# Last four token tiles of an attention and routed-spline kernel: one statistics pass, turned signs and keys from TensorE, sums on ScalarE, fp32r limits

## The reference

```
y   = (x1 - mean) / sqrt(var + 1e-5)                 # first norm
xf  = (y - mean(y)) * rsqrt(var(y) + 1e-5) * gamma + beta   # second norm
tile_scores    = sign(xf) @ tile_sigs.T              # 64 tiles of 16 features, signs of mean slopes
cluster_scores = sign(xf) @ cluster_sigs.T           # 8 clusters of 8 tiles
tile_idx = best tile inside the best cluster         # one tile per token
x_slice  = the 16 features of xf in that tile
mn, mx   = min and max of x_slice over ALL tokens that chose the same tile
u   = clip((x_slice - mn) / (mx - mn + 1e-8), 0, 1 - 1e-6)
gi  = int(u * 16)                                    # spline cell, 16 per feature
delta = (bases[tile, j, gi] + slopes[tile, j, gi] * (u * 16 - gi)) * scale[tile]
out = x1 + y, with delta added at the 16 features of the token's tile
```

## Time and profile before

| what | us |
|---|---|
| median of 3 runs | 3238.69 |
| lowest and highest | 3235.26, 3240.01 |
| the profiled execution | 3238.15 |
| its span, first to last instruction | 3236.4 |
| TensorE busy in the span | 3069.6 (95%) |
| VectorE busy | 2083.3 (64%) |
| ScalarE busy | 1490.6 (46%) |
| GpSimd busy | 714.7 (22%) |

### The profile page before, as it was taken

How to read it: one execution, slowest core, us unless ns; L and a number is a source line. 1 busy time by engine, 2 the same in 40 slices (tenths; PEclk the granted TensorE clock), 3 DMA queues, 4 the chain that set the end, 5 groups by cost and what they waited for, 6 DMA issues and landing times.

```text
span 3236.4 us, 39942 instructions
## 1 busy us (share of the span) xinstructions
PE 3069.6 (95%) x13890; PEld 2386.5 (74%) x13890; DVE 2083.3 (64%) x4440; ACT 1490.6 (46%) x2907; POOL 714.7 (22%) x516
## 2 busy tenths in 40 slices
PE   7999999999999999999999999999999999999924
PEld 4788768887788867888678876888678876888722
DVE  2555537775577746777377764777467763777687
ACT  2655525553445435445264543555345452555411
POOL 5222241112211131110411113111311113111046
PEclk9999999999999999999999999999999999999955
DMA  6554444444534445433454444444454444544301
GB/s 205 195 172 160 173 163 164 136 140 148 192 121 140 140 156 189 134 128 130 156 193 140 140 146 172 141 140 140 141 181 140 140 131 150 186 140 137 118 27 4
DMA packets 170054, 473.34 MB, mean 146 GB/s; under 512 B 33136, under 2 KB 61424, under 8 KB 149248
## 3 DMA queue, kind: packets, MB, share of 16 engines
q1 hardware_dynamic: 164784, 469.91, 43.7%
q0 software_dynamic: 5072, 0.88, 0.6%
HBM read 369.84 MB, written 67.31 MB: 135 GB/s over the span
## 4 chain that ended last, share of the span: by engine, by line
PE 83%; DVE 7%; issue 4%; ACT 3%; POOL 2%; DMA 1%; SPq 0%; DVEq 0%; ACTq 0%; POOLq 0%
PE psC L1934 18%; PE psD L1927 10%; PE psA L1864 8%; PE psT L1916 6%; PE psA L1833 5%; PE psB L1873 5%; PE psD L1884 4%; PE psS L1901 3%; PE psB L1833 3%; PE psS L1907 3%; PE psS L1903 3%; PE psS L1902 3%; PE psS L1904 3%; PE psA L1855 2%; PE psB L1855 2%
## 5 line engine op out<-in xcount | busy, mean ns | idle before, releaser
L1934 PE MATMUL psC<-w_o_pair,attn_hi 128*128 128x512 f32 x1920 | 638.4, 413 | 18.7 <-DVE acc L1342 10.8
L1033 ACT ACTIVATE exps_ring<-exps_ring,neg_max 128x512 f32<-128x512 f32 x512 | 370.8, 724 | 424.9 <-DVE neg_max L1314 424.9
L1314 DVE CUSTOM_DVE_ANT_0 exps_ring<-psS,mask 128x512 f32<-128x512 f32 x512 | 353.2, 690 | 294.4 <-PE psS L1907 289.1
L1044 ACT ACTIVATE probsT_hi<-psT 128x512 fp32r<-128x512 f32 x512 | 305.8, 599 | 364.9 <-PE psT L1916 363.3
L1934 PEld LDWEIGHTS psC<-w_o_pair,attn_hi 128*128 128x128 f32 x1920 | 332.2, 189 | 89.5 <-DVE acc L1342 24.9
L1039 ACT ACTIVATE exps_ring<-exps_ring,row_sum_inverse 128x512 f32<-128x512 f32 x512 | 369.6, 722 | 61.0 <-DVE row_sum_inverse L1320 61.0
L1326 DVE TENSOR_TENSOR probsT_lo<-psT,probsT_hi 128x512 fp32r<-128x512 f32 x512 | 350.6, 686 | 58.3 <-ACT probsT_hi L1044 56.6
L1934 PE MATMUL psC<-w_o_pair,attn_lo 128*128 128x512 f32 x960 | 379.4, 395 | 0.0
L1342 DVE TENSOR_TENSOR acc<-acc,psC 128x512 f32<-128x512 f32 x448 | 303.2, 677 | 17.3 <-PE psC L1934 11.4
L1916 PE MATMUL psT<-ident,exps_ring 128*128 128x128 f32 x2048 | 305.0, 272 | 0.0
L1916 PEld LDWEIGHTS psT<-ident,exps_ring 128*128 128x128 f32 x2048 | 252.8, 139 | 66.4 <-issue 2.1
(11 more groups left out here) (301 smaller groups left out, 5497.8 us busy)
## 6 DMA issues: line engine op xcount, KB each, us to landing
w_o_pair<-w_o_split SPq DMA_DIRECT2D x112, 1024.0 KB, 5.4
w_uq_ring<-w_uq_split SPq DMA_DIRECT2D x114, 384.0 KB, 3.5
w_uv_quad<-w_uv_split SPq DMA_DIRECT2D x29, 1024.0 KB, 5.0
w_uk_ring<-w_uk_split SPq DMA_DIRECT2D x114, 256.0 KB, 2.8
w_qr_sorted<-w_qr_split SPq DMA_DIRECT2D x29, 768.0 KB, 4.3
x_stage<-in_x_dram SPq DMA_DIRECT2D x32, 512.0 KB, 5.9
x_stage<-in_ctx_dram SPq DMA_DIRECT2D x32, 512.0 KB, 4.1
acc<-in_x_dram SPq DMA_DIRECT2D x32, 512.0 KB, 5.3
```

The lines of the kernel that those rows point to most:

```text
L1033: act.activation(E[:, qt, :], E[:, qt, :], ACT.Exp, scale=-1.0, bias=mx[:, i % 2, qt:qt + 1], accum_out=rs[:, i % 2, qt:qt + 1]).then_inc( ...
L1044: act.activation(PT[0][:, :, qt * P:(qt + 1) * P], psT[qt % 2][:, :].rearrange("p (c n) -> p c n", c=TT), ACT.Copy)\
L1314: dve.tensor_tensor_reduce(E[:, qt, :], psS[qt % 2][:, :], mask[:, qt, :], -SCALE, BIG, ALU.add, ALU.min, mx[:, i % 2, qt:qt + 1]).then_in ...
L1934: mm_ = pe.matmul(ps[:, :], attn[a][:, 2 * pair + i, t * P:(t + 1) * P], WO[:, half, o, i, :], start=i + a + o == 0, stop=i + a == 2)
```

## The change

All of it is in the ending.

- **One statistics pass.** As the mean of y is 0 and its variance var / (var + eps), both roots together are the power -0.5 of var (1 + eps) + eps². `end_stats` makes both arguments, GpSimd takes both roots in one instruction of two elements and derives bias and scale in two small ones. ScalarE makes the twice normed row without gamma and beta (`end_normed`) straight from `acc`, and later the sum x1 + y (`end_sum`).
- **Signs from turned rows.** TensorE turns the normed row, 8 blocks of 128 features (`end_turn`), and ScalarE takes the sign of each block from PSUM with gamma and beta as per-partition scale and bias (`end_sign`, 8 instructions of 128 columns, bf16). Gamma, beta and the slope signs come as columns (`cols`, three loads of 1024 single elements each, and two small ones for `gbt`), issued by SyncE where the gamma spread was, earlier in the last batch.
- **Keys by TensorE.** `end_keys`: 16 bf16 matmuls of 8 columns with the signs as weights and `wkey` (made by GpSimd) as the moving side give the 64 keys, and VectorE adds the tie numbers and takes the maximum in one instruction. The last four one-hots are turned singly (`end_turn_onehot`), and a small fp32 matmul fetches the chosen tile's gamma and beta (`end_gamma_beta`), which VectorE applies to the 16 chosen features.
- **Order.** TensorE's one-hot turnings stand between the last projections. VectorE does all adds and statistics first, then choices and slices.
- **Limits in fp32r.** `tab` is split into a high and a low part side by side (`tabs`, 8 columns); one fp32r matmul for each token tile, in four groups; VectorE sums the two parts in `place`. Groups 1 to 3 stand between the spline rows.
- **Equality and deltas.** VectorE does the equality of the first four token tiles, ScalarE that of 4 to 7 and of groups 1 to 3. The deltas are finished after 1, 2, 4, 6 and 8 token tiles and then by four.

```diff
+            def end_rstd(t):
+                row = mv4[:, t, :]
+                pool.wait_ge(s_tile[t], 5)
+                pool.tensor_tensor(row[:, 4:6], row[:, 2:4], nhalf[:, :], ALU.pow).then_inc(s_trstd[t], 1)
+                pool.wait_ge(s_trstd[t], 1)
+                pool.tensor_scalar(row[:, 7:9], row[:, 4:6], row[:, 0:1], -1.0, ALU.mult, ALU.mult)\
+                    .then_inc(s_trstd[t], 1)
+                pool.tensor_scalar(row[:, 6:7], row[:, 4:5], 1.0, None, ALU.add).then_inc(s_trstd[t], 1)
...
+            c.do(pool.tensor_copy(blk[:, 0, :], rampi[:, 0:8]))
...
+            pool.wait_ge(s_cols, 80)
+            sign_wide = cols[:, 2, :].rearrange("p (c a) -> p c a", a=1).broadcast_to([P, DB, 8])
+            c.do(pool.tensor_scalar(wkey[:, :, 0, :], sign_wide, 4096.0, None, ALU.mult))
...
+            for t in range(TT):
+                end_rstd(t)
+            for t in range(TT):
+                end_select(t)
...
+            def end_normed(t):
...
+                act.wait_ge(s_trstd[t], 2)
+                act.activation(ends[t][1], acc[:, t, :], ACT.Identity, scale=mv4[:, t, 5:6],
+                               bias=mv4[:, t, 8:9]).then_inc(s_tw, 1)
...
             def end_sign(t):
-                act.wait_ge(s_tile[t], 11)
-                act.activation(ends[t][2], ends[t][1], ACT.Sign).then_inc(s_tsign, 1)
+                act.wait_ge(s_twt, t + 1)
...
+                for blk_ in range(DB):
+                    ps = stages_end[t][blk_ // 4]
+                    act.activation(signs[t % 2][:, blk_, :], ps[:, (blk_ % 4) * P:(blk_ % 4 + 1) * P], ACT.Sign,
+                                   scale=cols[:, 0, blk_:blk_ + 1], bias=cols[:, 1, blk_:blk_ + 1]).then_inc(s_tsign, 1)
...
+            onehot_turned(0, 1, 2, 3)
+            end_normed(0)
+            onehot_turned(4)
+            end_normed(1)
             end_sign(0)
-            onehot_turned(3, 4)
+            onehot_turned(5)
+            end_normed(2)
             end_sign(1)
-            onehot_turned(5, 6)
+            onehot_turned(6)
+            end_normed(3)
             end_sign(2)
+            end_onehot_turned(0)
             end_sign(3)
-            onehot_turned(7)
+            end_onehot_turned(1)
+            end_onehot_turned(2)
+            end_sum(0)
+            end_onehot_turned(3)
+            for t in range(1, TT):
+                end_sum(t)
...
             def end_choose(t):
                 c = ends_c[t]
...
+                dve.wait_ge(s_key, t + 1)
+                c.do(dve.tensor_tensor_reduce(key[:, :], key_bank(t)[:, 0:NT], tie[:, :], -1.0, BIG,
+                                              ALU.add, ALU.min, kmax[:, :]))
+                c.do(dve.tensor_scalar(oh4[:, t, :], key[:, :], kmax[:, 0:1], None, ALU.is_equal))
...
             def end_slice(t):
...
+                c.do(dve.tensor_scalar(cand[:, 2, :], hot, 1.0, -BIG, ALU.subtract, ALU.mult), wait=False)
+                dve.wait_ge(s_tpool[t], 1)
+                c.do(dve.tensor_reduce(wsl[:, :], ends[t][2].rearrange("p (t j) -> p j t", j=SLICE), AX.X, ALU.add))
+                dve.wait_ge(s_gbs, t + 1)
+                c.do(dve.tensor_tensor(xk, wsl[:, :], spare[:, 0:SLICE], ALU.mult))
+                c.do(dve.tensor_tensor(xk, xk, spare[:, SLICE:2 * SLICE], ALU.add))
...
+            for t in range(TT):
+                add_tile(t)
+                end_stats(t)
             end_choose(0)
             end_choose(1)
             end_slice(0)
+            end_choose(2)
             end_slice(1)
             end_choose(3)
             end_slice(2)
             end_slice(3)
...
+            c.do(dve.tensor_copy(tabs[:, 0:4], tab))
+            dve.tensor_tensor(tabs[:, 4:8], tab, tabs[:, 0:4].bitcast(F32), ALU.subtract).then_inc(s_lim, 1)
...
+            def token_limits(g):
+                if g >= 2:
+                    pe.wait_ge(s_cell, g - 1)
+                for k in range(8 * g, 8 * g + 8):
+                    at = (k - 8 * g) * 8
+                    mm_ = pe.matmul(limit_bank(g)[:, at:at + 8], ohT[0:NT, k * P:(k + 1) * P], tabs,
                                     start=True, stop=True)
                 mm_.then_inc(s_fin, 1)
...
+            out_last(0)
             pe.wait_ge(s_ohin, 16)
...
+            turn_onehot(0)
+            turn_onehot(1)
+            out_last(1)
+            turn_onehot(2)
+            turn_onehot(3)
+            out_last(2)
+            turn_onehot(4)
+            end_turn(0)
+            out_last(3)
+            turn_onehot(5)
+            end_turn(1)
+            end_keys(0)
+            turn_onehot(6)
+            end_turn(2)
+            end_keys(1)
+            end_turn(3)
+            end_turn_onehot(0)
+            end_keys(2)
+            end_gamma_beta(0)
+            end_turn_onehot(1)
+            end_keys(3)
+            end_gamma_beta(1)
+            end_turn_onehot(2)
+            end_gamma_beta(2)
...
             spline_row(0)
+            end_turn_onehot(3)
+            end_gamma_beta(3)
             spline_row(1)
             spline_row(2)
...
+            spline_row(3)
+            pe.wait_ge(s_tile[TT - 1], NE)
```

More of the change, by code:

```diff
@@ L85, in xattn_ffn_kernel @@
     NF = 25
+    NE = 17
     NL = 5
@@ L189, in xattn_ffn_kernel @@
         gb = fs
-        gb_end = xs[:, 1, :]
+        wkey = ssb[:, 0:2 * NT].rearrange("p (c w a) -> p c w a", w=2, a=NT // CLUSTERS)
+        signs = [mask[:, 2 * s:2 * s + 2, :].rearrange("p a n -> p (a n)").rearrange("p (c n) -> p c n", n=P)
+                 for s in range(2)]
         wkrt = wkrs[:, :, :, :, :, :].rearrange("p w s c a r -> p (w s c a r)")
@@ L1653, in end_scale @@
[L1653 to L1661 removed]
+                c.do(dve.tensor_scalar(mv4[:, t, 3:4], mv4[:, t, 1:2], 1.0 + LN_EPS, LN_EPS * LN_EPS,
+                                       ALU.mult, ALU.add), wait=False)
@@ L2066, in body @@
                 for t in range(TT):
-                    if t < TT - 2 or last:
+                    if last:
+                        continue
+                    if t < TT - 2:
                         out_end(b, t, 0)
@@ L2105, in spline_row @@
                 mm_.then_inc(s_gb, 1)
-            def token_limits(ps, tiles):
-                for k in tiles:
-                    mm_ = pe.matmul(ps[:, k * 4:k * 4 + 4], ohT[0:NT, k * P:(k + 1) * P].bitcast(F32), tab[:, :],
+            def token_limits(g):
[4 more added lines that the diff above has]
+                    mm_ = pe.matmul(limit_bank(g)[:, at:at + 8], ohT[0:NT, k * P:(k + 1) * P], tabs,
@@ L2110, in token_limits, with end_turn @@
                                     start=True, stop=True)
                 mm_.then_inc(s_fin, 1)
-            pe.wait_ge(s_ohin, 16)
-            for g in range(NTOK // 4 - 1):
-                turn_onehot(g)
-            pe.wait_ge(s_ge, 1)
+            def end_turn(t):
+                pe.wait_ge(s_tw, t + 1)
+                if t == 0:
+                    pe.wait_ge(s_sm, B * H * TT)
+                elif t == 2:
+                    pe.wait_ge(freeC, B * CN)
+                    pe.wait_ge(freeD, B * DN)
+                else:
+                    pe.wait_ge(s_tsign, 8 if t == 1 else 16)
+                for c in range(DB):
+                    mm_ = pe.transpose(stages_end[t][c // 4][:, (c % 4) * P:(c % 4 + 1) * P],
+                                       ends[t][1][:, c * P:(c + 1) * P], ident)
+                mm_.then_inc(s_twt, 1)
@@ new lines, in end_keys @@
+            def end_keys(t):
+                if t == 0:
+                    pe.wait_ge(s_iota, 14)
+                    pe.wait_ge(freeA, B * AN)
+                elif t == 1:
+                    pe.wait_ge(freeB, B * BN)
+                else:
+                    pe.wait_ge(s_tile[t - 2], 7)
+                pe.wait_ge(s_tsign, 8 * (t + 1))
+                for c in range(DB):
+                    for w in range(2):
+                        mm_ = pe.matmul(key_bank(t)[:, c * 8:c * 8 + 8], signs[t % 2][:, c, :], wkey[:, c, w, :],
+                                        start=w == 0, stop=w == 1)
+                mm_.then_inc(s_key, 1)
@@ new lines, in end_turn_onehot, with end_gamma_beta @@
+            def end_turn_onehot(t):
+                pe.wait_ge(s_tile[t], 7)
+                pe.wait_ge(s_ge, NTOK // 4 - 1 + t)
+                pe.transpose(psTb[0][0:NT, 0:P], oh4[:, t, :], identb[:, :]).then_inc(s_oht, 1)
+            def end_gamma_beta(t):
+                if t > 0:
+                    pe.wait_ge(s_tile[t - 1], 11)
+                pe.wait_ge(s_ge, NTOK // 4 + t)
+                pe.matmul(spare[:, 0:2 * SLICE],
+                          ohT[0:NT, (NTOK - TT + t) * P:(NTOK - TT + t + 1) * P].bitcast(F32), gbt[0:NT, :],
+                          start=True, stop=True).then_inc(s_gbs, 1)
```

256 lines of the change are left out of this document (111 added, 145 removed).

## The result

| kernel | median, us | runs | lowest and highest |
|---|---|---|---|
| before | 3237.57 | 4 | 3235.26, 3240.01 |
| after | 3201.60 | 4 | 3201.52, 3202.76 |

The ratio is 0.989, with a 95% interval of 0.9872 to 0.9907: faster by 1.1%, 36 us, well over the 4.75 us over which the runs of before spread.

What follows compares the result with a forecast made beforehand. VectorE was taken to carry the last four tiles, the path then moving to a relay bound by ScalarE. Savings of 27.3, 1.3 and 1.0 us, 29.6 off 3238.15, gave 3208.6, with 0.5 for the median 3209; range 3201 to 3222.

Steps and rivals of the forecast that it cites:

- A: The whole kernel, the way thought likeliest: 3209 us, own range 3203 to 3215, chance 0.61.
- R: End of the last update of the running minima and maxima, 3146.29 before; forecast at 3119, 27.3 us earlier.
- The relay's start: Last four tiles, work handed from GpSimd through ScalarE and TensorE to VectorE: ScalarE starts tile 0's pass at 3080.9.
- Stretched steps, +3.9: VectorE's slices of the last four tiles: two mask steps held by GpSimd's long products, +3.9 us, range 0 to 7.6.
- Stage 2: Minima and maxima turned, first limits, first eight tiles placed: 8.43 us before, forecast 7.1.
- Stage 3: From the first eight tiles placed to the ninth scatter's start, VectorE making spline values and deltas: 32.0 us before, forecast 31.0.
- Stage 4: From the ninth scatter to the span's end, GpSimd alone setting the pace: 49.7 us, left alone by the change.
- Stage 1: The last four tiles, carried by VectorE: 75.01 us before, forecast 47.7.
- Rival C: Last four tiles without stretching or waiting, limits at 0.11 us each: time 3202, chance 0.10.
- Rival B: Last four tiles, waiting at each hand-over, TensorE at 1.2 GHz from 3083, two more stretched steps: 3221, chance 0.20.
- D: Slower: gamma, beta and slope signs, loaded as 3072 single elements, hold up GpSimd's roots; 3249 at 75 us, chance 0.03.
- E: ScalarE's equality lots starve the gathers, 64 columns as dear as 128, ninth scatter 4 us later: 3215, chance 0.05.

Runs made afterwards that it cites:

- wide signs: Against the kernel after: signs of the last four tiles without gamma and beta, two instructions of 512 columns instead of eight of 128; profiled time 3199.51 us.
- ScalarE relieved: Against the kernel after: ScalarE's pass over tile 0 goes ahead of one-hot copies 2 and 3, VectorE makes copies 4 to 6; profiled time 3200.67 us.
- the second mask step above: Against the kernel after: each slice's mask step made twice, the second after the first has ended; profiled time 3207.39 us.

## Why the prediction came out as it did

The forecast of 3209 was built on the right stages and the right relay, and it is 7.4 us long. That the range held owes something to luck. By the ending alone (37.8 us off 3238.15, and 0.5 for the median) the time would have been 3200.9, just below 3201, and A's own range, from 3203, was missed. By its own steps:

- **VectorE alone would allow R near 3105.** Not reached, as forecast: the path moved to the relay. Confirmed by the wide signs (3.1 us less) and by ScalarE relieved (1.6 less).
- **The relay's start.** Tile 0's pass was forecast for 3080.9 and began at 3083.08, which is 3080.7 in the old trace's time. The copies of one-hots 2 and 3 stood ahead of it as said. The root of two elements took 0.74 us where 1.07 or less was taken.
- **ScalarE's own work to the end of tile 2's signs**, forecast at 15.7 us, was 14.5: eight signs take 2.76 us (0.345 each, not 0.385), the one-hot copies 0.48. This term was 1.2 too large.
- **The waits**, put at 2 us, were 1.3: one wait, for a one-hot turning behind tile 2's projections (the 1.30 in ScalarE's first rows above). Behind it ScalarE never waited up to 3098.86. The reason feared did not come: from 3083 to 3098 the granted clock averaged 0.97, where it had been 0.75, with TensorE busy 11.5 us of these 15 instead of 9.0, so it ran at 2.4 GHz for nearly all of the stretch. In the old stretch at the same distance from the ending's start the clock was 0.83:

```profile
3080.64:3095.64 15.00, 9.67 (x49) 6.25 (x48) 13.31 (x18) 3.57 (x6) 5.23 (x4) 0.83 0.00 0
```

With the turnings moved behind the projections, it was 1.2 GHz from 3090 to 3100, and the eight turnings of tile 0 took 1.97 us instead of 1.09.
- **Keys, gamma and beta.** From the signs' end to VectorE's first step with gamma and beta 1.7 us went by (3098.86 to 3100.59), with 2.7 forecast. Sixteen key matmuls take 0.54 to 0.57 us, not 1.6 to 3.2:

```profile
3091.15 0.55 PE L2175 MATMUL psA<-slope_sign_b,mask 128*128 128x8 bf16 x16
```

This term was mis-sized by a row of another kind: it was priced by turnings of 128 columns, and these move 8.
- **From there VectorE sets R**, 13.7 us forecast, 13.6 measured (3100.59 to 3114.19).
- **Stretched steps, +3.9: this step failed.** None of the four mask steps was held (the range given for the term, 0 to 7.6, did include that). In the trace of before the held one stood behind the start of GpSimd's product; in the new order both come after the same one-hot, and VectorE, which goes straight on in its own queue while GpSimd waits for a semaphore, was 0.04 or 0.05 us ahead each time:

```profile
3102.75 0.20 DVE L1714 TENSOR_SCALAR candidates<-end_onehot 128x64 f32<-128x64 bf16 x1
...
3106.93 0.20 DVE L1714 TENSOR_SCALAR candidates<-end_onehot 128x64 f32<-128x64 bf16 x1
```

```profile
3102.79 1.92 POOL L913 TENSOR_TENSOR room_of_probsT<-room_of_values,end_onehot 128x1024 f32<-128x1024 f32 x1 [4.95 <-DVE end_onehot L1709]
3106.97 1.92 POOL L913 TENSOR_TENSOR room_of_probsT<-room_of_probsT,end_onehot 128x1024 f32<-128x1024 f32 x1 [2.26 <-DVE end_onehot L1709]
```

I had asked whether a product begins where a slice begins, and not which of the two comes first. By the second mask step above the price was right, 1.79 us for each one held. The Trainium skill (SBUF — State Buffer, Who interferes with whom) has whichever instruction starts first take the shared port for its whole length; these runs agree for VectorE's step, with 0.20 us ahead and 1.79 us behind. That GpSimd is held in its turn they don't show: its product took 1.92 us just behind a mask step and 1.91 with none beside it (3093.28). Against the forecast's reading of the page, a mask step first in the slice was what kept it free here.

- **Stage 2**, 7.1 forecast, 7.07 measured; eight limits took 1.86 us with 1.75 taken. The Trainium skill (TensorE: Matmul & The Clock Gate, LDWEIGHTS) gives about 107 ns for the load of 128 weight columns; at the granted clock of 0.50, 1.2 GHz, of this stretch, instructions stood over 0.2 us apart, twice that, in both forms (eight weight loads took 1.77 us), and the 0.9 us more that would have followed did not come.
- **Stage 3**, 31.0 forecast, 30.08 measured. VectorE waited 0.76 us for ScalarE's equality instead of 2.5, but also 1.48 us for spline row 6 (1.3 forecast, as hidden):

```profile
3136.32 0.69 DVE L1800 TENSOR_TENSOR rope_term<-psS,acc 128x512 f32<-128x512 f32 x1 [1.48 <-PE psS L2137]
...
3140.23 0.69 DVE L1800 TENSOR_TENSOR cosT<-psD,acc 128x512 f32<-128x512 f32 x1 [0.76 <-ACT acc L1278]
```

Three more lots of deltas were put at 2.3 us; removing the early ones gave back 0.85.
- **Stage 4** as forecast: 49.66 us, scatters 1.85 apart.

Stage 1's error adds up: 0.2 from the start, 1.2 and 0.7 on ScalarE, 1.0 from the keys, 0.1, and 3.9 from the stretched steps, 7.1 of 7.2. Rival C came true in what it says of stage 1, no stretching and hardly any waiting, not in its limits at 0.11; it had been given 0.10 on the strength of the one stretched row. That its 3202 was met so closely is luck: limits 0.9 us dearer than it had them and a body that may be longer stand against signs and keys 2.2 us cheaper. Rival B had the clock wrong. D fell early: the single elements of gamma, beta and the slope signs landed 5.4 to 6.2 us after issue, long before the first root. E's condition, 64 columns as dear as 128, did not hold (3.98 against 4.90 us for sixteen).

Left open is the body. By the medians the time fell by 36.0 us and the ending by 37.8, so the body may be 1.8 longer, which is less than the 4.75 us over which the runs of before spread; nothing was run to settle it.

## What to carry to other kernels

When work is taken off the engine that carries a stage, follow the chain through the hand-overs and add up the one engine that never waits in it; here that was ScalarE, and its relief paid in full, also together with the earlier series of scatters. Where two engines start from the same semaphore and contend for one port, ask which issues first: here the short step that was next in its own queue went free in 0.20 us, and the same step a place later was held for 1.79, nearly the other's whole length. An ending in which one engine plays out a fixed series (scatters at 1.85 us) is shortened only by bringing forward the point from which that series no longer starves.

## What the runs showed of the hardware

- Sixteen bf16 key matmuls of 8 columns with 128 by 128 weights took 0.55 us at a granted clock near 1.00 (at 3091) and 0.57 us at 0.50 (at 3102): about 0.035 us each, hardly a matter of the clock. The fp32r and fp32 ones of 8 columns with 64 by 128 weights took 0.22 to 0.23 us each at 0.50. So the bf16 matmul was over six times cheaper here; the rows of the weights (128 against 64) differ too, and no run separates the type from the rest.
- The hold of VectorE's step by a product of GpSimd is not tied to the mask step. In the kernel with wide signs the one-hot step (64 keys, fp32 to bf16) began 0.24 us behind a product of GpSimd and took 1.72 us instead of 0.25:

```profile
3093.51 1.72 DVE L1709 TENSOR_SCALAR end_onehot<-tile_key,key_max 128x64 bf16<-128x64 f32 x1
```

- A pass with two per-partition operands from PSUM costs ScalarE 0.345 us for 128 columns; eight of them took 2.86 us, two instructions of 512 columns without operands 1.06.
